# A recurrent layer and a quantised MLP on one core: chunk 0's norm and the gates' weights by halves, and three steps moved in the last chunks

## The reference, cut to what matters

```
x = x + attn(layernorm(x));  x = x + ffn(layernorm(x))

attn: pre = x @ W + b;  i, f, o, z = split(pre, 4)      # W is 256 x 1024
      i = 10*tanh((i + input_bias)/10);  f = -softplus(f)
      step: m' = max(f + m, i);  c = exp(f+m-m')*c + exp(i-m')*tanh(z)
            n = exp(f+m-m')*n + exp(i-m');  h = sigmoid(o) * c/(n + 1e-6)
      out = h / sqrt(mean(h*h) + 1e-8) * scale
ffn:  y = silu(layernorm2(x) @ dequant(fc1) + b1);  x + 0.5*(y @ dequant(fc2) + b2)
```

## Time and profile before

| | |
|---|---|
| median of three runs | 306.15 us |
| the profiled execution | 304.67 us |
| its span, first to last instruction | 302.9 us |
| PE busy | 293.1 us (97%) |
| DVE busy | 256.4 us (85%) |
| ACT busy | 235.7 us (78%) |
| POOL busy | 131.4 us (43%) |

### The profile page before, as it was taken

How to read it: one execution, slowest core, us unless ns; L and a number is a source line. 1 busy time by engine, 2 the same in 40 slices (tenths; PEclk the granted TensorE clock), 3 DMA queues, 4 the chain that set the end, 5 groups by cost and what they waited for, 6 DMA issues and landing times.

```text
span 302.9 us, 4764 instructions
## 1 busy us (share of the span) xinstructions
PE 293.1 (97%) x1728; PEld 254.8 (84%) x1728; DVE 256.4 (85%) x470; ACT 235.7 (78%) x382; POOL 131.4 (43%) x133
## 2 busy tenths in 40 slices
PE   7899999999999899999999999999999989999996
PEld 5688788877898689968899889988799888889896
DVE  3999887999999799999997899698999899683521
ACT  2688988799989974999693994979884978866910
POOL 3052045001098419911993129601698777135000
PEclk9999999799999999999999999999999999999999
DMA  7990003000000422043004400240000552302201
GB/s 261 344 335 0 0 0 72 0 0 2 0 1 2 70 70 72 0 92 118 0 3 69 139 2 0 36 106 0 0 3 2 102 106 55 51 35 55 52 35 69
DMA packets 15206, 17.87 MB, mean 59 GB/s; under 512 B 832, under 2 KB 14416, under 8 KB 15056
## 3 DMA queue, kind: packets, MB, share of 16 engines
q1 hardware_dynamic: 10368, 12.07, 11.6%
q0 software_dynamic: 4400, 4.73, 9.6%
q10 hardware_dynamic: 416, 0.79, 0.7%
HBM read 8.67 MB, written 4.19 MB: 42 GB/s over the span
## 4 chain that ended last, share of the span: by engine, by line
DVE 35%; POOL 23%; PE 22%; issue 15%; DMA 3%; ACT 0%; POOLq 0%; DVEq 0%; SPq 0%
POOL rows L1195 6%; POOL g L1180 4%; DVE y_lo L898 4%; DVE g L866 3%; PE mm_ps L260 3%; PE mm_ps L258 3%; PE mm_ps L259 3%; DVE rows L874 3%; DVE bn L879 3%; POOL r L1188 3%; DVE rec L822 2%; DVE rec L807 2%; DMA rows<-x 2%; POOL rrms L1166 2%; PE z_ps L355 2%
## 5 line engine op out<-in xcount | busy, mean ns | idle before, releaser
L355 PE MATMUL z_ps<-w_hi,y_hi 128*128 128x256 f32 x200 | 57.3, 286 | 0.9 <-DVE rows L912 0.6
L357 PE MATMUL z_ps<-w_hi,y_lo 128*128 128x256 f32 x200 | 56.3, 282 | 0.0
L356 PE MATMUL z_ps<-w_lo,y_hi 128*128 128x256 f32 x200 | 56.3, 282 | 0.0
L614 ACT ACTIVATE y<-mm_ps,b_all,unit 128x512 f32<-128x512 f32 x58 | 44.6, 768 | 3.8 <-PE mm_ps L349 3.1
L898 DVE TENSOR_TENSOR y_lo<-y,y_hi 128x512 fp32r<-128x512 f32 x56 | 38.5, 707 | 6.2 <-ACT y_hi L617 6.2
L342 PE MATMUL mm_ps<-gt_hi,w_hi 128*128 128x512 f32 x124 | 39.8, 402 | 0.3 <-ACT y L606 0.3
L355 PEld LDWEIGHTS z_ps<-w_hi,y_hi 128*128 128x128 f32 x200 | 37.7, 188 | 1.7 <-DVE rows L912 0.8
L349 PE MATMUL mm_ps<-gt_lo,w_hi 128*128 128x512 f32 x124 | 38.9, 395 | 0.0
L258 PE MATMUL mm_ps<-xt_hi,wg_hi 128*128 128x512 f32 x96 | 38.4, 400 | 0.0
L356 PEld LDWEIGHTS z_ps<-w_lo,y_hi 128*128 128x128 f32 x200 | 37.7, 189 | 0.3
L259 PE MATMUL mm_ps<-xt_lo,wg_hi 128*128 128x512 f32 x96 | 37.9, 395 | 0.0
(11 more groups left out here) (203 smaller groups left out, 732.2 us busy)
## 6 DMA issues: line engine op xcount, KB each, us to landing
rows<-b_bc POOLq DMA_DIRECT2D x8, 512.0 KB, 5.1
out<-rows SPq DMA_DIRECT2D x15, 256.0 KB, 2.1
rows<-x SPq DMA_DIRECT2D x7, 512.0 KB, 6.6
q<-fc_q SPq DMA_DIRECT2D x2, 1024.0 KB, 11.3
wg_raw<-fc_scales SPq DMA_DIRECT2D x1, 1024.0 KB, 8.5
wg_raw<-w_gates SPq DMA_DIRECT2D x1, 512.0 KB, 5.8
wg_raw<-w_gates ACTq DMA_DIRECT2D x1, 512.0 KB, 6.1
w_lo<-q POOLq DMA_DIRECT2D x1, 512.0 KB, 4.6
```

Source lines behind the costliest of these rows:

```text
L355: pe.matmul(dst, hi, w2_hi[:, k], start=(k == 0), stop=False)
L356: pe.matmul(dst, hi, w2_lo[:, k], start=False, stop=False)
L357: return pe.matmul(dst, lo, w2_hi[:, k], start=False, stop=(k == KF - 1))
L614: act.activation(y[:, j % YBUFS], fc1_bank(c, j), ACT.Silu, bias=b1_all[:, j:j + 1], scale=unit[:, j:j + 1]).then_inc(silu_done, 1)
```

## The change

Four edits. First, chunk 0's norm goes by halves: `first_ln1` takes sums, means and the two small tiles for the token tiles 0 and 1, and then the same for 2 and 3; POOL (`first_ln1_root`) takes a root of 128x2 for each half; `first_x_normalised(u)` normalises a half as soon as its root is there. Second, the gates' weights go by halves of their columns: four DMAs of 256 KB in place of two of 512 KB, four ACT roundings of 128x512, four DVE low parts. The low parts of the first half (the gate tiles 0 to 3) stand between and behind the halves of the norm, those of the second half behind `x_low(0)`, and the fifth gate tile waits for them. SP's wait ahead of the DMA of `fc2_scales` counts four low parts.

Third, around chunk 6's norm, DVE takes `y_low(5, 1)` ahead of `h_scaled(6)` and `final(4, 1)` ahead of `residual(6)`; around chunk 7's, `y_low(6, 4)` ahead of `ln2_sums(7)`. Fourth, PE does five blocks of chunk 5's token tile 1 ahead of `g_turned(6)`, where it did four, and three behind.

```diff
-            sp.dma_start(wg_raw[:, 0], w_gates[0:P, :]).then_inc(wg_in[0], 16)
+            for u in range(2):
+                sp.dma_start(wg_raw[:, 0, u * T:(u + 1) * T], w_gates[0:P, u * T:(u + 1) * T]).then_inc(wg_in[u][0], 16)
...
-            sp.wait_ge(wg_split_lo, KD)
+            sp.wait_ge(wg_split_lo, 2 * KD)
...
+                    if c == 0 and j == 4:
+                        pe.wait_ge(wg_split_lo, 2 * KD)
...
-            fc2(5, [1], range(0, KF // 2))
+            fc2(5, [1], range(0, 5))
             g_turned(6)
-            fc2(5, [1], range(KF // 2, KF))
+            fc2(5, [1], range(5, KF))
...
+            for u in range(2):
+                for k in range(KD):
+                    act.wait_ge(wg_in[u][k], 16)
+                    act.activation(wg_hi[:, k, u * T:(u + 1) * T], wg_raw[:, k, u * T:(u + 1) * T], ACT.Copy
+                                   ).then_inc(wg_split_hi, 1)
...
+            def first_ln1():
+                dve.wait_ge(x_half_landed, 16)
+                for n in range(2):
+                    dve.bn_stats(bn1[:, n], rows[:, 0, n]).then_inc(first_stat, 1)
+                dve.wait_ge(first_stat, 2)
+                for n in range(2):
+                    dve.bn_aggr(mv1[:, n], bn1[:, n]).then_inc(first_stat, 1)
+                dve.wait_ge(first_stat, 4)
+                dve.tensor_scalar(ve1[:, 0, 0:2], mv1[:, 0:2, 1], EPS_LN, None, ALU.add).then_inc(first_stat, 1)
+                dve.tensor_scalar(nm1[:, 0, 0:2], mv1[:, 0:2, 0], -1.0, None, ALU.mult).then_inc(first_stat, 1)
...
+            def first_ln1_root():
+                halves = slice(0, 2), slice(2, TT)
+                for u, stat, count, r in ((0, first_stat, 6, first_r), (1, ln1_stat, 10, ln1_r)):
+                    pool.wait_ge(stat, count)
+                    pool.tensor_tensor(r1[:, 0, halves[u]], ve1[:, 0, halves[u]], minus_half[:, halves[u]], ALU.pow
+                                       ).then_inc(r, 1)
+                    pool.wait_ge(r, 1)
+                    pool.tensor_tensor(nr1[:, 0, halves[u]], nm1[:, 0, halves[u]], r1[:, 0, halves[u]], ALU.mult
+                                       ).then_inc(r, 1)
...
-            ln1(0)
-            x_normalised(0)
-            for k in range(KD):
-                dve.wait_ge(wg_split_hi, k + 1)
-                dve.tensor_tensor(wg_lo[:, k], wg_raw[:, k], wg_hi[:, k].bitcast(F32), ALU.subtract
-                                  ).then_inc(wg_split_lo, 1)
-            x_low(0)
+            first_ln1()
+            first_x_normalised(0)
+            wg_low(0, 0)
+            first_x_normalised(1)
+            wg_low(0, 1)
+            x_low(0)
+            for k in range(KD):
+                wg_low(1, k)
...
-            y_low(5, range(0, 1))
+            y_low(5, range(0, 2))
             h_scaled(6)
             final(4, 0)
-            y_low(5, range(1, 3))
+            y_low(5, range(2, 3))
+            final(4, 1)
             residual(6)
-            final(4, 1)
...
-            y_low(6, range(2, 4))
+            y_low(6, range(2, 5))
             ln2_sums(7)
-            y_low(6, range(4, 5))
             ln2(7)
```

More of the change, by code:

```diff
@@ L183, in layer @@
         ident_ready, half_ready, zeros_ready = sem("ident_ready"), sem("half_ready"), sem("zeros_ready")
-        wg_in = [sem(f"wg_in{k}") for k in range(KD)]
+        wg_in = [[sem(f"wg_in{u}{k}") for k in range(KD)] for u in range(2)]
         q1_in, q2_in, s1_in, s2_in, col_in, row_in, b2_in = (sem(n) for n in (
@@ L619, in _ @@
             act.dma_start(rows[:, 0, 2:TT], x_view[0, 0, :, 2:TT]).then_inc(x_landed[0], 16)
-            act.dma_start(wg_raw[:, 1], w_gates[P:2 * P, :]).then_inc(wg_in[1], 16)
+            for u in range(2):
+                act.dma_start(wg_raw[:, 1, u * T:(u + 1) * T], w_gates[P:2 * P, u * T:(u + 1) * T]
+                              ).then_inc(wg_in[u][1], 16)
             act.preload_act_table_set("sigmoid_and_others")
-            for k in range(KD):
-                act.wait_ge(wg_in[k], 16)
-                act.activation(wg_hi[:, k], wg_raw[:, k], ACT.Copy).then_inc(wg_split_hi, 1)
+            for u in range(2):
+                for k in range(KD):
+                    act.wait_ge(wg_in[u][k], 16)
+                    act.activation(wg_hi[:, k, u * T:(u + 1) * T], wg_raw[:, k, u * T:(u + 1) * T], ACT.Copy
+                                   ).then_inc(wg_split_hi, 1)
             x_high(0)
@@ L743, in ln1_sums @@
                 b = c % XBUFS
[L744 to L747 removed]
+                dve.wait_ge(x_landed[b], at(c // XBUFS, 16, 16))
                 for n in range(TT):
[L749 to L750 removed]
                     dve.bn_stats(bn1[:, n], rows[:, b, n]).then_inc(ln1_stat, 1)
@@ L762, in ln1_means, with first_x_normalised, wg_low @@
                 dve.tensor_scalar(nm1[:, s], mv1[:, :, 0], -1.0, None, ALU.mult).then_inc(ln1_stat, 1)
+            def first_ln1():
[8 more added lines that the diff above has]
+                dve.tensor_scalar(nm1[:, 0, 0:2], mv1[:, 0:2, 0], -1.0, None, ALU.mult).then_inc(first_stat, 1)
+                dve.wait_ge(x_landed[0], 16)
+                for n in range(2, TT):
+                    dve.bn_stats(bn1[:, n], rows[:, 0, n]).then_inc(ln1_stat, 2)
+                dve.wait_ge(ln1_stat, 4)
+                for n in range(2, TT):
+                    dve.bn_aggr(mv1[:, n], bn1[:, n]).then_inc(ln1_stat, 2)
+                dve.wait_ge(ln1_stat, 8)
+                dve.tensor_scalar(ve1[:, 0, 2:TT], mv1[:, 2:TT, 1], EPS_LN, None, ALU.add).then_inc(ln1_stat, 1)
+                dve.tensor_scalar(nm1[:, 0, 2:TT], mv1[:, 2:TT, 0], -1.0, None, ALU.mult).then_inc(ln1_stat, 1)
+            def first_x_normalised(u):
+                if u == 0:
+                    dve.wait_ge(first_r, 2)
+                else:
+                    dve.wait_ge(ln1_r, 2)
+                for n in range(2 * u, 2 * u + 2):
+                    dve.tensor_scalar(xn[:, n], rows[:, 0, n], r1[:, 0, n:n + 1], nr1[:, 0, n:n + 1],
+                                      ALU.mult, ALU.add).then_inc(xn_done, 1)
+            def wg_low(u, k):
+                half = slice(u * T, (u + 1) * T)
+                dve.wait_ge(wg_split_hi, u * KD + k + 1)
+                dve.tensor_tensor(wg_lo[:, k, half], wg_raw[:, k, half], wg_hi[:, k, half].bitcast(F32), ALU.subtract
+                                  ).then_inc(wg_split_lo, 1)
             def ln1(c):
```

12 lines of the change are left out of this document (3 added, 9 removed).

## The result

| | before | after |
|---|---|---|
| median | 305.46 us (six runs) | 303.5 us (six runs, 303.37 to 303.87) |
| profiled execution | 304.67 us | 303.46 us |
| its span | 302.9 us | 301.7 us |
| mean granted clock, share of 2.4 GHz | 0.994 | 0.994 |

What follows compares the result with a forecast made beforehand. PE was taken as the bound nearly everywhere, set by its start and later waits. 0.82 us at the start plus 0.46 in the last chunks, 1.28, took 306.15 to 304.9 us; range of 8 in 10: 304.4 to 305.9.

Steps and rivals of the forecast that it cites:

- the last of the sum: Whole kernel: profiled 304.67 would go to 303.4; from the median of 306.15, 1.5 above it, minus 1.28 gives 304.9.
- D: Rival at the start: PE's clock falls on the first gate products, costing up to 1.8 us, 306.7; chance 0.05.
- The start: First 14 us: first gate product 0.46 earlier and 0.36 saved behind it, together 0.82 us.
- The root of 128x2: POOL, chunk 0's norm: 0.20 fixed and the rest going with the columns, 0.62 us; the second root 6.61 to 7.33.
- the weights: Loads at the start: all four halves landing only at 7.4 would take away the 0.46; not expected, same bytes, same queues.
- Rival A: POOL at the start: the root's time doesn't go with the columns; start gives -0.08 to 0.36, time 305.5; chance 0.20.
- The rule on GpSimd and VectorE: Start: by this rule wg_low(0, 0) beside the second root makes the second half 0.4 later, start's gain about 0.4.
- The head start passes in full: Middle of the kernel: the start's gain lasts, since DVE waits 1.52 us before 49.98 on what follows PE.
- The last chunks: Chunks 6 and 7 norms: 0.60 kept at y's sixth low part, less 0.02 and 0.12, sum 0.46 us.
- The means of chunk 7: DVE, chunk 7's second norm: means 1.44 after their sums' start, 0.13 later with y_low(6, 4) ahead; edit costs 0.12.
- The step of h(7): DVE, late: h(7) gains only 0.25, ready at 258.50 where PE wants it at 258.48; costs 0.02, meeting within 0.1.

Runs made afterwards that it cites:

- long ones: Runs of a kernel with a mean granted clock of 0.988 or 0.989; 1.2 to 1.6 us longer; for the kernel before 305.78 to 306.74 us.
- short ones: Runs of a kernel with a mean granted clock of 0.993 or more; for the kernel before 304.27 to 305.06 us.
- start_only: Kernel before with only the start's edits (chunk 0's norm and the gates' weights by halves): -0.35 us [-0.51, -0.21] against the kernel before.
- high_first: Changed kernel, but ACT rounds the turned x ahead of the weights' second halves: -1.30 us [-1.40, -1.15] against the kernel before.
- tail_only: Kernel before with only the edits of the last chunks: -0.72 us [-0.86, -0.55] against the kernel before.

## Why the prediction was wrong, step by step

**The step that failed** is the last of the sum: "carried over to the median of the runs, which stands 1.5 above it". The 1.5 was taken for a part of every run, which a change leaves as it is. It is the distance of two groups of runs. The three runs shown ahead have 306.00 to 306.26; their clock isn't on record, but of the 98 runs of before all above 305.7 are long ones. The changed kernel's six runs were all short ones (clock 0.994). 304.67 - 1.28 = 303.39 would have been 0.1 from the median of 303.5. No case of the prediction had this, D least of all: D had the clock fall at a new place, and it was falling at an old one. The row was there: 0.97 for 48.6 to 110, and I used it for what a fall would cost, not to ask whether it was the same in every run. That the sum itself came out at 303.4 is partly luck: its start was too large by 0.3 and its last chunks too small by 0.1 to 0.2, and over the short runs on one chip the change gave 0.99 (0.75 to 1.08), less than the 1.28.

**The start**, 0.82 forecast, is 0.54 in the profile and 0.35 (0.21 to 0.51) by the runs of `start_only`, whose own profile has 0.41. The root of 128x2 took 0.73 and not 0.62: with 1.05 for 128x4 that makes an estimate of 0.41 fixed and 0.16 a column, from one duration of each size. The second took 0.81 and its product ended at 7.80, where I had 7.69 (with 0.08 for the product beyond its 0.20 that the prediction doesn't name); the last tile was normalised at 8.57, where I had 8.47. That is 0.10 of the 0.29 missing at the first gate product. Most of the rest is what I had weighed and dismissed, the weights: their first halves were rounded by 7.48, but ACT then waited until 8.15 for the second ones, was busy with them until 9.3 and took x at 9.20, 0.14 after the transposes' end at 9.06. "ACT is free at about 8.2" was wrong by 1.1. The DMA rows, as the earlier trace rows:

```profile
wg_raw<-w_gates SPq DMA_DIRECT2D x2, 256.0 KB, 5.6
wg_raw<-w_gates ACTq DMA_DIRECT2D x2, 256.0 KB, 6.1
```

Each is the middle of two. On SP's queue the first half landed 4.8 after its issue and the second, issued 0.5 later, 6.4 after its own, so the second halves were there at 8.1 and 8.3, later than the whole loads (7.05 and 7.37): that the same bytes passed the same queues didn't keep them at 7.4. With whole loads ACT had rounded from 7.07 to 9.08 without a wait, now the second halves hold it until 8.15. Why they land later is open. The wait at 12.45 went, as forecast. Rival A was partly right: the root's price lies between mine and its own, and the 0.35 by the runs lies in its span for the start (-0.08 to 0.36), though half of what was missing came from ACT.

**The rule on GpSimd and VectorE.** The trace has root 0.81 with the two-input instruction beside its end and 0.80 without, product 0.35 and 0.20. The Trainium skill, "GPSIMD Engine Reference", section "Specifications", says that the two contend when a VectorE instruction has two SBUF inputs. The product agrees; the price at this place was 0.15 (0.26 in `high_first`), not the 0.4 that I had worked out from the spread of the roots; the root next to it shows none.

**The head start passes in full**: right. 0.54 at 12.72, 0.53 at DVE's step (49.98 to 49.45), 0.58 at the transposes of h (131.51 to 130.93).

**The last chunks**, 0.46 forecast, 0.53 to 0.65 in the profile (1.19 at PE's last wait, less a head start of 0.54 at 12.72 or 0.66 at 242, where PE starts on the block at 241.57 and not 242.23) and 0.72 (0.55 to 0.86) by the runs of `tail_only`, whose own profile has 0.54 at the same wait. PE's wait for the final sum went, and the next one was for y's sixth low part, as said. In `tail_only`, where there is no head start, it came 0.78 earlier (246.53 for 247.31), not 0.60. I had priced the tile that moves ahead of `h_scaled(6)` at 0.60, the distance of two such tiles; at its old place the two tiles took 1.49 together, one of them 0.88. POOL was at work beside them; that it is the reason isn't shown. The means of chunk 7 stood 1.44 behind their sums, to the hundredth as forecast, and that edit cost 0.12 to 0.20, with 0.12 forecast. The step of h(7) on DVE came 1.07 earlier, of which 0.54 is the head start: 0.53 and not the 0.25 of the forecast. It ended at 257.64, and the transposes of h began at 257.72, so they did meet within 0.1.

**D** didn't happen at the start: the changed kernel's clock is 1.00 from 9 to 13 us and from 13.0 to 48.6.

## What to carry to other kernels

Before a difference of one execution is carried over to a median, see which group of runs that execution belongs to: here one number, the mean granted clock, told 0.994 from 0.989 and was worth more than the whole change. Here a train of 16 products with one moving column counted as busy in every view, and yet the clock fell behind it in 159 of 192 runs; 31 idle columns more cost nothing, left it up in 34 of 51 runs and kept the fall short in 16. And where one operand's preparation is split into halves, look at what the second half then stands in front of: splitting the weights gave 0.36 on DVE and took it back on ACT, until ACT took x first.
